# Attention scores as full fp32 products on 64 rows, even and odd heads in the two row halves, eight heads a burst

## The reference

```python
xn = layernorm(x)                                  # per token, 256 features
q, k, v = xn @ w_q, context @ w_k, context @ w_v   # 1024 columns = 16 heads x 64
sim = einsum('bhid,bhjd->bhij', q, k) * 64 ** -0.5
out = einsum('bhij,bhjd->bhid', softmax(sim), v)
x = x + out @ w_o + b_o
y = layernorm(x)
gate = softmax(y @ gate_w); keep the two largest, made to sum to 1
x = x + sum over experts of gate_e * (relu(y @ W1_e + b1_e) @ W2_e + b2_e)
```

## Time and profile before

| | us |
|---|---|
| median of 3 runs | 1632.73 |
| lowest, highest | 1630.2, 1637.94 |
| profiled execution, span | 1630.7 |
| PE busy | 1602.2 (98%) |
| DVE busy | 1437.7 (88%) |
| ACT busy | 1200.5 (74%) |
| POOL busy | 820.2 (50%) |

### The profile page before, as it was taken

How to read it: one execution, slowest core, us unless ns; L and a number is a source line. 1 busy time by engine, 2 the same in 40 slices (tenths; PEclk the granted TensorE clock), 3 DMA queues, 4 the chain that set the end, 5 groups by cost and what they waited for, 6 DMA issues and landing times.

```text
span 1630.7 us, 45315 instructions
## 1 busy us (share of the span) xinstructions
PE 1602.2 (98%) x13604; PEld 1524.8 (94%) x13605; DVE 1437.7 (88%) x4180; ACT 1200.5 (74%) x3485; POOL 820.2 (50%) x950
## 2 busy tenths in 40 slices
PE   7999999999999999999999999999899999999997
PEld 6899999999999999999999999999899999999997
DVE  6899999999999999999999999999788777777775
ACT  5777777777777777777777777777676767777774
POOL 4244444455444445544444554445546555555555
PEclk9999999999999999999999999999999999999998
DMA  6421211112221111222111122211489755555554
GB/s 184 126 85 68 71 59 58 58 65 85 71 71 58 58 58 65 82 74 71 58 58 58 63 79 78 71 58 45 165 266 270 152 88 85 87 86 88 88 83 61
DMA packets 106444, 145.06 MB, mean 89 GB/s; under 512 B 12768, under 2 KB 88672, under 8 KB 106144
## 3 DMA queue, kind: packets, MB, share of 16 engines
q1 hardware_dynamic: 60944, 89.00, 17.1%
q0 software_dynamic: 26816, 37.32, 13.0%
q10 hardware_dynamic: 18640, 18.19, 4.1%
HBM read 77.09 MB, written 67.38 MB: 89 GB/s over the span
## 4 chain that ended last, share of the span: by engine, by line
issue 47%; POOL 20%; DMA 11%; PE 8%; DVE 7%; DVEq 2%; ACT 2%; POOLq 1%; ACTq 1%; SPq 0%
DMA out<-stage_room,number 10%; POOL lists L655 7%; PE bank_a L1420 3%; POOL prob L662 3%; POOL rstd L641 2%; DVE stage_room L1365 2%; POOL stage_room L705 2%; DVE hid L1348 2%; POOL stage_room L701 2%; PE bank_s L1420 1%; DVEq L1360 1%; POOL out L741 1%; PE bank_v L1453 1%; DVEq L1339 1%; ACT xst_h L865 1%
## 5 line engine op out<-in xcount | busy, mean ns | idle before, releaser
L662 POOL TENSOR_TENSOR prob<-prob,inv 128x512 f32<-128x512 f32 x256 | 271.1, 1059 | 569.0 <-DVE inv L965 568.3
L783 ACT ACTIVATE prob<-bank_s,low 128x128 f32<-128x128 f32 x1024 | 362.4, 369 | 113.5 <-DVE low L960 109.4
L741 POOL DMA_INDIRECT out<-stage_room,number x142 | 230.2, 1621 | 53.8 <-issue 53.1
L776 ACT ACTIVATE probt<-bank_t 128x512 f32<-128x512 f32 x256 | 152.9, 597 | 82.5 <-PE bank_t L1427 81.6
L783 ACT ACTIVATION_READ_ACCUMULATOR prob<-bank_s,low 128x1 f32 x1024 | 212.1, 207 | 0.0
L960 DVE TENSOR_REDUCE low<-bank_s 128x4 f32<-128x512 f32 x256 | 175.6, 686 | 34.8 <-PE bank_s L1420 31.4
L1071 DVE SCALAR_TENSOR_TENSOR stage_room<-xin,wo_t 128x256 f32<-128x256 f32 x480 | 178.9, 426 | 0.0
L987 DVE TENSOR_TENSOR kt_l<-bank_a,kt_h 64x512 fp32r<-64x512 f32 x256 | 172.9, 675 | 3.7 <-ACT kt_h L800 1.9
L894 ACT ACTIVATE hidt_h<-hid 128x512 fp32r<-128x512 f32 x142 | 89.7, 632 | 116.0 <-DVE hid L1348 114.2
L1427 PE MATMUL bank_t<-ident,prob 128*128 128x128 f32 x1024 | 154.0, 273 | 4.8 <-POOL prob L662 4.5
L1420 PE MATMUL bank_s<-kt_l,qt_h 128*128 128x256 f32 x512 | 157.6, 308 | 0.0
(11 more groups left out here) (237 smaller groups left out, 5386.5 us busy)
## 6 DMA issues: line engine op xcount, KB each, us to landing
stage_room<-lists ACTq DMA_DIRECT2D x67, 265.0 KB, 2.9
halves<-stage_room SPq DMA_DIRECT2D x32, 512.0 KB, 4.2
homes<-halves SPq DMA_DIRECT2D x16, 1024.0 KB, 5.9
xin<-in_x SPq DMA_DIRECT2D x32, 256.0 KB, 2.8
stage_room<-in_x SPq DMA_DIRECT2D x32, 256.0 KB, 3.3
stage_room<-in_w SPq DMA_DIRECT2D x32, 256.0 KB, 4.3
out<-stage_room SPq DMA_DIRECT2D x32, 256.0 KB, 2.2
cin<-in_ctx SPq DMA_DIRECT2D x32, 128.0 KB, 2.5
```

Source lines behind the costliest of these rows:

```text
L662: pool.tensor_tensor(prob[:, n % 4, :, :], prob[:, n % 4, :, :], wide(inv[:, n % 4, :], P), ALU.mult).then_inc(s_norm.sem, 1)
L741: pool.indirect_dma_start(out, bass.IndirectOffsetOnAxis(ap=number[:, u, b:b + 1], axis=0), ysum[:, u, b, :], None, compute_op=ALU.add).th ...
L776: act.activation(probt[:, n % 2, :, :], bank_t[:, :].rearrange("p (h q) -> p h q", h=4), ACT.Copy).then_inc(t_copy.sem, 1)
L783: e = act.activation(prob[:, n % 4, h, :], bank_s[n % 2][:, h * P:(h + 1) * P], ACT.Exp, bias=low[:, n % 4, h:h + 1], scale=-1.0, accum_ou ...
```

## The change

Queries and keys are kept once, in fp32, without low parts. `kt` is packed, with no zeros: even heads in rows 0 to 63, odd heads in rows 64 to 127. `scores` runs at even n only and makes a burst of eight fp32 products, for two units at once: each takes 64 rows (one half), 128 weight columns and 128 moving columns, in turn from the even and the odd half. The even heads of the burst go to `bank_s[0]`, the odd ones to `bank_s[1]`, so a unit is now the four even or the four odd heads of eight, and `values` picks its heads by that. The burst waits for the exponentials of both units before it, and for ACT's copies of keys and queries. DVE has no part in q and k any more; bank reuse after them goes by `a_hi` (`bank_before`). In the order of products k01 comes before v00, and DVE copies v00 one step later. `zero_keys` is gone.

```diff
@@ -116,8 +116,8 @@
         [("o1", FROM0), ("t0", NEXT)],
         [("v10", CUR), ("v11", CUR)],
         [("q00", NEXT), ("k00", NEXT)],
-        [("q01", NEXT), ("v00", NEXT)],
-        [("f0", BOTH), ("k01", NEXT), ("v01", NEXT)],
+        [("q01", NEXT), ("k01", NEXT)],
+        [("v00", NEXT), ("f0", BOTH), ("v01", NEXT)],
     ]
 
     A_SLOTS_LAST = A_SLOTS[:4] + [[], [("v10", CUR)], [("v11", CUR)], [("f0", BOTH)]]
...
@@ -125,19 +125,20 @@
 
     OUT_SLOTS = [
         [("v01", NEXT)],
-        [("q10", CUR), ("k10", CUR)],
+        [],
         [("o0", PREV)],
-        [("k11", CUR), ("q11", CUR), ("o1", FROM0)],
+        [("o1", FROM0)],
         [("t0", NEXT), ("v10", CUR), ("v11", CUR)],
-        [("q00", NEXT)],
-        [("k00", NEXT), ("q01", NEXT), ("v00", NEXT)],
-        [("f0", BOTH), ("k01", NEXT)],
+        [],
+        [],
+        [("v00", NEXT), ("f0", BOTH)],
     ]
-    OUT_SLOTS_LAST = OUT_SLOTS[:4] + [[("t0", NEXT)], [("q00", NEXT)], [("v10", CUR)], [("v11", CUR), ("f0", BOTH)]]
+    OUT_SLOTS_LAST = OUT_SLOTS[:4] + [[], [], [("v10", CUR)], [("v11", CUR), ("f0", BOTH)]]
     A_EVENTS = [e for slot in A_SLOTS for e in slot]
     A_BANKS = 4
     assert len(A_EVENTS) % A_BANKS == 0
     HI_EVENTS = [e for e in A_EVENTS if e[0][0] in "tqk"]
+    DONE_EVENTS = [e for e in A_EVENTS if e[0][0] not in "qk"]
     UNITS = [(f"u{n}", CUR) for n in range(8)]
 
     LATE = [("u6", PREV), ("u7", PREV)] + [(f"u{n}", CUR) for n in range(6)]
...
@@ -224,8 +225,9 @@
             cin = place("cin", 2, 2 * P)
             xn = place("xn", 2, D)
             place("not_used", WORK + HOME - taken_to[0])
-            qt = [place(f"qt_{s}", 2, CHUNKS // 2, 2 * P, dt=F32R) for s in "hl"]
-            kt = [place(f"kt_{s}", 2, 2, CHUNKS // 2, 2, P, dt=F32R) for s in "hl"]
+            qt = place("qt", 2, CHUNKS // 2, 2 * P)
+            kt = place("kt", 2, 2, CHUNKS // 2, P)
+            place("not_used_1", WORK + 4 * HOME - taken_to[0])
             assert taken_to[0] == WORK + 4 * HOME
             vv = place("vv", 2, 2, HALF * HEAD)
             prob = place("prob", 4, 4, P)
...
@@ -289,10 +291,9 @@
 
 
             w_hi, w_lo = sem("w_hi"), sem("w_lo")
-            zeroed = sem("zeroed")
             x_in, c_in, r_in, x1_out = sem("x_in"), sem("c_in"), sem("r_in"), sem("x1_out")
             sent = sem("sent")
-            a_full, a_done = signal("a_full", A_EVENTS), signal("a_done", A_EVENTS)
+            a_full, a_done = signal("a_full", A_EVENTS), signal("a_done", DONE_EVENTS)
             a_hi = signal("a_hi", HI_EVENTS)
             c_hi, c_lo = signal("c_hi", [("c", NEXT)]), signal("c_lo", [("c", NEXT)])
             s_full, s_low, s_exp = signal("s_full", UNITS), signal("s_low", UNITS), signal("s_exp", UNITS)
...
@@ -366,6 +367,16 @@
                     it = PAIRS - 1
                     here = a_full.present(it)
                 return bank_a[(a_full.before(it if isinstance(it, int) else 2) + here.index(name)) % A_BANKS]
+
+            def bank_before(it, name):
+
+                if not isinstance(it, int):
+                    names = [n for n, _ in A_EVENTS]
+                    k = names.index(name) - A_BANKS
+                    return (it if k >= 0 else it - 1), names[k]
+                order = [(j, n) for j in range(-1, PAIRS + 1) for n in a_full.present(j)]
+                k = order.index((it, name)) - (A_BANKS - 1 if (it, name) == (PAIRS, "f0") else A_BANKS)
+                return order[k] if k >= 0 else (it, None)
 
             STATIC = 4 * STEPS
             LOOPED = TILES // STEPS * STEPS
...
@@ -706,18 +716,6 @@
                                            bo[:, :].rearrange("p (o d) -> p o d", o=1).to_broadcast([P, 2, D]),
                                            ALU.add).then_inc(pool_step.sem, 1)
 
-                def zero_keys():
-
-
-                    wait(pool, ln1_step, -1, "ln1")
-                    for side in range(2):
-                        part = slice((1 - side) * HEAD, (2 - side) * HEAD)
-                        for s in range(2):
-                            pool.memset(kt[s][part, :, :, :, side, :].bitcast(F32), 0.0).then_inc(zeroed, 1)
-
-                        pool.wait_ge(zeroed, 2 * (side + 1))
-
-
                 pool.iota(tile_no[:, :], [[1, EARLY]], base=0, channel_multiplier=0,
                           allow_small_or_imprecise_dtypes=True).then_inc(numbered, 1)
                 pool.iota(half_no[:, 1:], [[1, (TILES + 1) // 2], [0, 2]], base=0, channel_multiplier=0,
...
@@ -792,14 +790,11 @@
                     if kind == "t":
                         last = act.activation(xt[0][:, 0:DC, :], src[:, :].rearrange("p (c t) -> p c t", c=DC), ACT.Copy)
                     elif kind == "q":
-                        last = act.activation(qt[0][:, int(name[1]), 2 * k:2 * k + 2, :],
+                        last = act.activation(qt[:, int(name[1]), 2 * k:2 * k + 2, :],
                                               src[:, :].rearrange("p (c t) -> p c t", c=2), ACT.Copy, scale=-SCALE)
                     else:
-                        for side in range(2):
-                            part = slice(side * HEAD, (side + 1) * HEAD)
-                            last = act.activation(
-                                kt[0][part, int(name[1]), :, 2 * k:2 * k + 2, side, :],
-                                src[part, :].rearrange("p (c b t) -> p b c t", c=2, b=2), ACT.Copy)
+                        last = act.activation(kt[:, int(name[1]), :, 2 * k:2 * k + 2, :].rearrange("p b c t -> p c b t"),
+                                              src[:, :].rearrange("p (c b t) -> p c b t", c=2, b=2), ACT.Copy)
                     last.then_inc(a_hi.sem, 1)
 
                 def numerators(it, sums):
...
@@ -967,25 +962,13 @@
                 def second_part(it, name):
                     src = a_bank(it, name)
                     kind, k = name[0], int(name[-1])
-                    if (kind in "tqk"):
+                    if kind == "t":
                         wait(dve, a_hi, it, name)
                     else:
                         wait(dve, a_full, it, name)
                     if kind == "t":
                         last = dve.tensor_tensor(xt[1][:, 0:DC, :], src[:, :].rearrange("p (c t) -> p c t", c=DC),
                                                  xt[0][:, 0:DC, :].bitcast(F32), ALU.subtract)
-                    elif kind == "q":
-                        g = int(name[1])
-                        last = dve.scalar_tensor_tensor(qt[1][:, g, 2 * k:2 * k + 2, :],
-                                                        src[:, :].rearrange("p (c t) -> p c t", c=2), -SCALE,
-                                                        qt[0][:, g, 2 * k:2 * k + 2, :].bitcast(F32),
-                                                        ALU.mult, ALU.subtract)
-                    elif kind == "k":
-                        for side in range(2):
-                            part = slice(side * HEAD, (side + 1) * HEAD)
-                            at = (part, int(name[1]), slice(None), slice(2 * k, 2 * k + 2), side, slice(None))
-                            last = dve.tensor_tensor(kt[1][at], src[part, :].rearrange("p (c b t) -> p b c t", c=2, b=2),
-                                                     kt[0][at].bitcast(F32), ALU.subtract)
                     elif kind == "v":
                         last = dve.tensor_copy(vv[:, int(name[1]), k, :], src[:, :])
                     elif kind == "o" and isinstance(it, int) and it == 0:
...
@@ -1428,17 +1416,17 @@
                     last.then_inc(t_full.sem, 1)
 
                 def scores(it, n):
+
                     g, b = n // 4, (n % 4) // 2
-                    if n % 4 < 2:
-
-                        wait(pe, a_done, it if g else it - 1, "q11" if n == 5 else f"k{g}{n % 4}")
-                    wait(pe, s_exp, it, f"u{n}", 2)
-                    for k in range(2):
-                        c = 2 * (n % 2) + k
-                        last = three(bank_s[n % 2][:, k * 2 * P:(k + 1) * 2 * P],
-                                     [qt[s][:, g, c, b * P:(b + 1) * P] for s in range(2)],
-                                     [kt[s][:, g, b, c, :, :].rearrange("p s k -> p (s k)") for s in range(2)], True, True)
-                    last.then_inc(s_full.sem, 1)
+                    wait(pe, a_hi, it if g else it - 1, "q11" if g else "k01")
+                    wait(pe, s_exp, it, f"u{n + 1}", 2)
+                    for c in range(CHUNKS // 2):
+                        for side in range(2):
+                            part = slice(side * HEAD, (side + 1) * HEAD)
+                            last = pe.matmul(bank_s[side][:, c * P:(c + 1) * P], qt[part, g, c, b * P:(b + 1) * P],
+                                             kt[part, g, b, c, :], start=True, stop=True, skip_group_check=True)
+                            if c == CHUNKS // 2 - 1:
+                                last.then_inc(s_full.sem, 1)
 
```

(10 more changed lines are left out.)

33 lines of the change are left out of this document (17 added, 16 removed).

## The result

The changed kernel takes 1583.75 us (median of 4 runs, 1581.79 to 1586.61), the kernel before 1631.58 in 4 runs (its median with the runs beside it). The ratio is 0.9703, with a 95% interval of 0.968 to 0.9727: 48 us faster. The forecast was 1593 us, 9 us too high. The profiled executions have spans of 1584.8 and 1630.7 us, 45.9 apart.

What follows compares the result with a forecast made beforehand. PE alone was taken as the bound: 0.96 + 0.15 = 1.11 us a burst against 1.42 saves 0.31, 40 us over 128 bursts; 1630.7 - 40 + 1 = 1592 us span, forecast 1593, range 1567 to 1700 (own case 1567 to 1626).

Steps and rivals of the forecast that it cites:

- PE sets the pace, and a microsecond on it counts 32 times: Attention pairs: PE busy 35.72 of 35.72 us, so a microsecond saved on PE in every pair is worth 32.
- Removed: 1.42 us a burst: Scores on PE: two units, twelve one-pass products, 1.42 us gone per burst, four bursts a pair, 128 in all.
- Added: eight steps: Scores on PE: eight fp32 products per burst with row halves overlapping, eight steps of 0.12 us, 0.96 us.
- The switch: 0.15 us: PE between burst and transposes: one new change of array division, 0.15 us, bounds 0 and 0.2.
- DVE's and ACT's relief: worth 0: Each pair: DVE loses 8.1 us and ACT 2.3 us, both hidden under a full PE, worth 0.
- the tight place: Ahead of scores at 599.98: exponentials end 0.2 us before; blamed on DVE's low parts from 601.39, which go away.
- the wait: Ahead of each burst: PE now waits for the exponentials of both units of the burst before; cost taken as 0.
- The order of products: worth 0: k01 before v00, v00's copy a step later on DVE: same instructions, banks freed four products ahead, worth 0.
- The single set of score banks: Rival, ahead of bursts: late exponentials bind; 0.3 us late at each gives today's time; shares partial overlap's case, chance 0.07.
- The last pair: +1 us of loss: Last pair: little work between the bursts, so 1 us of loss was allowed.
- No overlap (1699 or 1716): Rival, inside each burst: row halves don't overlap, 67 or 83 us slower; chances 0.12 (loads) and 0.11 (streams too).
- The speedup for row tiles: Burst on PE: skill page's 3.07 times for four row tiles gives 1.40 us with the switch, no gain.

Runs made afterwards that it cites:

- the experiment: Changed kernel, but DVE still makes the unread low parts of queries and keys, and banks are reused only after it is done with them: 1622.91 us, ratio 0.9947.
- the last experiment: Changed kernel with the old order of products (v00 in step 6, k01 in step 7) and DVE's gate_top ahead of v00's copy: 1585.24 us, ratio 0.9724.

## Why the prediction was right, point by point

- *PE sets the pace, and a microsecond on it counts 32 times.* Right: PE is full in both windows, and every edit that lengthened the burst or its switches came back in the period (0.54, 0.10, 0.32 and 0.20 us per burst, against four times that per pair).
- *Removed: 1.42 us a burst.* Right; the whole exchange adds up to the 0.39 us of the period only with it.
- *Added: eight steps.* The overlap is right, and with it the choice of the earlier trace rows as the nearest row. The step was taken at 0.12 us; it is 0.112. This term was 0.06 us too large: 0.90 us instead of 0.96, which is 8 us in 128 bursts. It is most of the miss in a burst, 0.31 us forecast against 0.39, or 10 us in 128. That the forecast of the time is off by 9 us too is in part chance: the pairs outside the steady loop brought 4 us less than the rate of the loop, the 1 us allowed for the last pair was not needed, and the medians lie 2 us further apart than the profiled spans (10 - 4 + 1 + 2 = 9). I had both numbers, 0.112 for loads alone and 0.12 for 256 columns together with their loads, and took the pace of products twice as wide. The run with half the columns shows that at 128 columns the load sets the pace.
- *The switch: 0.15 us.* Right in size. From the last step's end (0.10 + 8 x 0.112 = 1.00 us after the burst's start) to the effective start of the transposes (587.31 - 586.16 = 1.15) is 0.15 us, and a whole extra switch costs 0.20.
- *DVE's and ACT's relief: worth 0.* Right alone (1630.84 us) and misleading as a term. With the new bursts and DVE's low parts in the places of the experiment, 39 of the 48 us are lost. The prediction did say that the tight place was tight for a cause that goes away, and it kept 0 for the wait; it did not price what happens if the cause stays. The rows that it gives for the cause are also those of another place: the low parts at 601.39 stand ahead of the minima of u0, while the exponentials that end at 599.78 are u7's. It should have stood in the sum as a condition: 3.4 us of DVE work ahead of the minima of u7, against 1.07 us of slack there.
- *The order of products: worth 0.* Right for the order, as the last experiment shows. But the reason I gave (the same instructions, banks freed four ahead) doesn't cover it: what decides is what stands behind a waiting copy on DVE, and 1.5 us a pair hung on that. By the prediction's reason either order would have done; that the changed kernel has the one that avoids this wait was luck.
- *The single set of score banks.* Not binding: 2.3 us of waits in all, 2.2 of them at one burst of the first pair, and 0.40 us of slack at the tightest place of the steady pairs. It binds once DVE is late.
- *The last pair: +1 us of loss.* Wrong in sign and small: the stretch from the last pair's first transposes to the end is 512.0 us against 513.2.
- *No overlap (1699 or 1716).* It did not come about in this order. With one half behind the other it comes a little over halfway: 1650.7.
- *The speedup for row tiles.* The Trainium skill (TensorE: Matmul & The Clock Gate, Measured speedup) gives 3.07 times for four tiles, and the estimate from it was 1.40 us a burst and no gain. Eight steps of 0.112 for 16 records are twice the pace of one by one: two halves overlap in full here.

## What to carry to other kernels

Put products on the two row halves in turn, one by one, and price them by the step of a load (0.112 us for 128 fp32 columns of weights) once the moving operand has 128 columns or fewer; count 0.15 to 0.20 us for each change of how the array is divided, and keep such groups next to each other. An engine that is off the critical path is worth nothing alone, but look at each new wait for what stands ahead of its producer there: here 3.4 us of DVE work in one place decided over some 40 us, and 4.4 us a pair elsewhere over nothing. An instruction that waits for PE doesn't belong ahead of a chain that PE needs.

## What the runs showed of the hardware that I had not expected

- Records of one row half start ahead of records of the other half that come before them in the program: with four products of a half in a run, six records had started 0.58 us into the burst and nine at 0.86, where one by one gives five and seven. The bursts of fours, threes and twos fit with three waiting records passed (1.71, 1.48 and 1.26 us worked out, 1.71, 1.49 and 1.26 measured). The Trainium skill (TensorE: Matmul & The Clock Gate, Part 3, in what overlaps and what doesn't) has matmuls start and end strictly in program order; the starts in these traces don't agree. In all these bursts each half signals its own last product, so nothing relies on the order between the halves.
- The first step of a row half is 0.10 us longer with 128 moving columns and 0.05 with 64, in the middle of a burst too (by halves, 0.21 us at 0.55). Its load starts with its record and not 0.11 us ahead, as those of all later records of the half do.
- Runs of two products cost 0.10 us more than products in turn: the load of the odd half's fifth record starts at 0.55 us instead of 0.45. Why three records can be passed and not four is open.
